# Softmax attention: maxima of four heads side by side in four PSUM banks, and the work between the scores dealt out anew

## The reference, cut to what matters

```python
q = (x @ w_q + b_q).reshape(B, Lq, 16, 32)          # x: 8 x 512 x 512
k = (context @ w_k + b_k).reshape(B, -1, 16, 32)    # context: 8 x 512 x 384
v = (context @ w_v + b_v).reshape(B, -1, 16, 32)
scores  = einsum('bqhd,bkhd->bhqk', q, k) / sqrt(32)
weights = softmax(scores, axis=-1)
out = einsum('bhqk,bkhd->bqhd', weights, v).reshape(B, Lq, 512) @ w_o + b_o
```

## Time and profile before

| | |
|---|---|
| median of 3 timed runs | 1717.89 us (1717.18 to 1721.56) |
| the profiled execution | 1716.18 us, its span 1713.9 us |
| softmax attention | from about 622 us to about 1420 us of the span |
| busy over the span | PE 92%, DVE 72%, ACT 66%, POOL 60% |
| mean granted TensorE clock | 0.977 of full |

### The profile page before, as it was taken

The page is one execution under the profiler, slowest core; times in us unless marked ns, Lnnn a source line. Parts: engine busy times, 40 slices in busy tenths (PEclk is TensorE's granted clock), DMA queues, the critical chain, the costliest instruction groups (busy, mean ns, idle before and its releaser), DMA issues. The chain is left out here.

```text
span 1713.9 us, 29296 instructions
## 1 busy us (share of the span) xinstructions
PE 1576.5 (92%) x8836; PEld 711.7 (42%) x8836; DVE 1225.9 (72%) x1756; ACT 1128.4 (66%) x1895; POOL 1023.3 (60%) x738
## 2 busy tenths in 40 slices
PE   5999878998999977999999999999999978999998
PEld 3545433444444432334344443444343413444443
DVE  4978898997989745776776767676767666665553
ACT  5667598887888744665656666666656566566562
POOL 4767437766677723565667566665757565554452
PEclk9989999999999997999999999999999999999999
DMA  8411000000000112121211212121211100010001
GB/s 313 143 66 42 1 1 1 1 1 1 0 1 1 62 52 73 33 59 26 58 33 38 54 29 57 26 57 32 58 25 40 55 25 25 25 49 24 24 24 49
DMA packets 61230, 72.21 MB, mean 42 GB/s; under 512 B 15312, under 2 KB 40784, under 8 KB 60624
## 3 DMA queue, kind: packets, MB, share of 16 engines
q1 hardware_dynamic: 56944, 62.22, 12.3%
q10 hardware_dynamic: 4192, 8.92, 1.3%
HBM read 37.40 MB, written 8.39 MB: 27 GB/s over the span
## 5 line engine op out<-in xcount | busy, mean ns | idle before, releaser
L1556 DVE TENSOR_REDUCE s_mx<-bank 128x1 f32<-128x512 f32 x512 | 336.9, 685 | 193.9 <-PE bank L1684 188.0
L1443 ACT ACTIVATE s_E<-bank 128x512 f32<-128x512 f32 x512 | 293.8, 595 | 195.4 <-PE bank L1696 171.9
L1342 POOL TENSOR_TENSOR s_E<-s_E 128x1024 f32<-128x1024 f32 x128 | 300.3, 2367 | 123.7 <-PE bank L1704 116.6
L1684 PE MATMUL bank<-s_KA,s_QA 96*128 96x512 f16 x512 | 193.3, 388 | 20.7 <-DMA s_KA<-sm_cx 10.4
L1696 PE MATMUL bank<-s_QA,s_KA 97*128 97x512 f16 x512 | 195.7, 384 | 3.9 <-ACT s_E L1443 1.4
L1335 POOL TENSOR_TENSOR sm_cx<-s_qkf,sm_cx 128x512 f16<-128x512 f32 x64 | 76.4, 1194 | 171.3 <-ACT sm_cx L1421 171.2
L1865 POOL TENSOR_TENSOR sm_cx<-m_xf,sm_cx 128x512 f16<-128x512 f32 x60 | 84.1, 1407 | 105.0 <-ACT sm_cx L1907 105.0
L1704 PE MATMUL bank<-s_E,s_V 128*32 128x512 f32 x1024 | 135.6, 602 | 3.9 <-ACT s_E L1443 3.9
L1075 PE MATMUL bank<-sm_zz,w1raw 128*128 128x512 f16 x256 | 99.7, 389 | 28.4 <-DVE sm_cx L962 15.4
L1098 PE MATMUL bank<-f_w2q,w2raw 128*128 128x512 f16 x512 | 121.8, 379 | 0.6 <-DVE w2raw L950 0.3
L772 POOL TENSOR_TENSOR sm_wkv<-sm_wkv,sm_cx 128x511 f32<-128x511 f32 x48 | 66.2, 1380 | 89.8 <-DVE sm_wkv L962 80.5
(11 more groups left out here) (264 smaller groups left out, 4055.1 us busy)
## 6 DMA issues: line engine op xcount, KB each, us to landing
sm_cx<-in_ctx SPq DMA_DIRECT2D x16, 768.0 KB, 4.6
s_QA<-sm_cx SPq DMA_DIRECT2D x384, 32.0 KB, 1.9
s_KA<-sm_cx SPq DMA_DIRECT2D x372, 32.0 KB, 1.9
X<-in_x SPq DMA_DIRECT2D x8, 1024.0 KB, 6.7
out_x<-X SPq DMA_DIRECT2D x8, 1024.0 KB, 4.3
w1raw<-in_w ACTq DMA_DIRECT2D x1, 4096.0 KB, 13.9
w2raw<-in_w ACTq DMA_DIRECT2D x1, 4096.0 KB, 27.3
w1raw<-in_wq SPq DMA_DIRECT2D x1, 1024.0 KB, 5.4
```

The costliest lines, as they stand in the source:

```text
L1342: e.tensor_tensor(into, into, other, ALU.add).then_inc(s_sum.sem, 1)
L1443: e.activation(E[:, SLOT[k] + h, :], SC[u % 2][:, :], ACT.Exp, scale=1.0 / float(np.sqrt(DH)))\
L1556: e.tensor_reduce(mx[:, h, q:q + 1], MX[q % 2][:, :], AX.X, ALU.max).then_inc(s_red.sem, 1)
L1684: e.matmul(MX[k % 2][:, :], QA[0:MROW, m, h, q * P:(q + 1) * P], KA[0:MROW, m, h, :], start=True, stop=True).then_inc(s_mx.sem, 1)
```

## The change

It is confined to the softmax attention.

1. **Maxima.** `maxima(b, m, q)` issues four matmuls, one for each head, that contract only over the 32 rows of the high halves, straight from `qkh` (now double buffered) rather than from the stacked `QA` and `KA`. They write banks 0 to 3. DVE reduces two banks at a time: 2 reductions of 128 x 2 x 512 for each query tile, 8 a group, where there were 16 of 128 x 512.
2. **Phases.** Banks 0 and 1 are also the score banks. So a group becomes four phases: when the four exponentials of a key tile are done, PE makes the next group's maxima of one query tile, DVE reduces banks 0 and 1, and then the scores of the next key tile may go. `attend` and `denominators` stand between maxima and scores.
3. **The maximum row** is transposed at the start of its own group rather than at unit 15 of the one before, and its DMA is issued by SP (`maximum_row`) and no longer by ACT.
4. **The rest** (`queries`, `values`, `output`, transposes, residuals, reciprocals, divisions, `summed`) is dealt out anew. Outputs are spread over `m == 1` and `m == 2`; the transposes go to units 9, 11, 13, 15.

```diff
-    SPARSE_K, SPARSE_V = (-1, 1, 3), (5, 7, 9, 12)
-    K_UNITS = (SPARSE_K, (-1, 0, 1), (2, 3, 4), SPARSE_K)
-    T_UNITS, STATS_UNITS = (4, 6, 8, 10), (1, 3, 6, 10)
-    RESIDUAL = {4: 0, 8: 1, 12: 2}
+    Q_AT = ((-1, -1, 1, 3), (-1, -1, 1, 3), (0, 1, 2, 3), (0, 1, 2, 3))
+    K_AT = ((3, 5, 7), (5, 7, 7), (7, 7.5, 11), (3, 3.5, 5))
+    T_AT = (9, 11, 13, 15)
+    O_AT = ({}, {3: ((0, 0),), 7.5: ((0, 1),), 11: ((0, 2), (0, 3)), 11.5: ((1, 0),), 13: ((1, 1),), 15: ((1, 2), (1, 3))},
+            {3: ((2, 0),), 5: ((2, 1),), 7: ((2, 2),), 9: ((2, 3),), 11: ((3, 0),), 11.5: ((3, 1),), 13: ((3, 2),), 15: ((3, 3),)},
+            {})
+    RES_AT = ({}, {12: 0}, {0: 1, 10: 2}, {0: 3})
...
+        SC, MX, MAXED, NUM, DEN, R6, R7 = banks[0:2], banks[0:4], pairs[0:2], banks[4], banks[5], banks[6], banks[7]
...
+            def maximum_row(b, m):
+                s_mrow.wait(e, b, m + 1)
+                s_sc.wait(e, b, 16 * (m + 1) - 16 * NG)
+                e.dma_start(QA[MROW:MROW + 1, m, :, :].rearrange("o h (q n) -> o (h q) n", n=P), mrow[:, :])\
+                    .then_inc(s_md[m].sem, 16)
+
             def step(b, m, first, last):
                 proj = what(b, m, first, last)[0]
                 if m == 0 and not last:
                     context(b + 1)
+                maximum_row(b, m)
                 if proj:
                     stack(e, *proj, 0)
                     stack(e, *proj, 1)
...
-            def maximum(b, m, k):
-                h, q = divmod(k, TT)
+            def maxima(b, m, q):
                 s_mT.wait(e, b, m)
-                s_mx.wait(e, b, 16 * m + k + 1)
-                e.tensor_reduce(mx[:, h, q:q + 1], MX[q % 2][:, :], AX.X, ALU.max).then_inc(s_red.sem, 1)
+                s_mx.wait(e, b, TT * m + q + 1)
+                for i in range(2):
+                    e.tensor_reduce(mx[:, 2 * i:2 * i + 2, q], MAXED[i][:, :, :], AX.X, ALU.max).then_inc(s_red.sem, 1)
...
+                s_red.wait(e, b, 2 * (TT * m + q))
+                high = qkh[m % 2]
+                for h in range(4):
+                    head = slice(h * DH, (h + 1) * DH)
+                    last = e.matmul(MX[h][:, :], high[head, 0, q * P:(q + 1) * P], high[head, 1, :], start=True, stop=True)
+                last.then_inc(s_mx.sem, 1)
...
+                if proj and Q_AT[m][0] < 0:
+                    queries(*proj, 0, 0)
+                rows(b, m)
+                between(-1)
+                for u in range(UNITS):
+                    t, h = divmod(u, 4)
+                    if nxt and h == 0:
+                        if t == 0:
+                            s_mrow.wait(e, b, m + 1)
+                        e.wait_ge(s_ex.sem, s_ex.count(b, 16 * m + 4 * t))
+                        maxima(*nxt, t)
+                    if t and h == 0:
+                        attend(b, m, t - 1)
+                    if div and u == 0:
+                        attend(*div, TT - 1)
+                        denominators(*div, 0)
+                    if div and u == 4 * DN_TILE[m]:
+                        denominators(*div, 1)
+                    between(u - 0.5)
+                    score(b, m, u, nxt)
+                    between(u)
```

More of the change, by code:

```diff
@@ L1367, in step @@
                     e.tensor_scalar(omu[:, :], mu[:, :], -1.0, 1.0, ALU.mult, ALU.add).then_inc(s_c, 1)
-                summed(b, m, 0, 0)
-                summed(b, m, 0, 1)
+                if m == 0:
+                    ln_p(e, b + 1)
+                if m != 2:
+                    summed(b, m, 0, 1)
+                if late and (m == 0 or m == 3 and not last):
+                    divided(*late)
                 if last and m == 3:
@@ L1486, in step @@
             def step(b, m, first, last):
-                proj, nxt, div = what(b, m, first, last)
-                if m == 2 and not last:
-                    for c in range(KC):
-                        context(b + 1, c)
-                if proj:
-                    queries(*proj, 0)
-                if div and N_UNIT[m] < 0:
+                proj, nxt, div, late = what(b, m, first, last)
+                rows(b, m)
+                if first and m == 0:
+                    e.wait_ge(s_lo, 2)
+                    e.wait_ge(s_raw[3], 32)
@@ L1494, in step @@
+                if m == 0 and not first:
+                    values(b, 1)
+                if m == 1:
+                    values(b, 3)
+                if m == 2 and not last:
+                    context(b + 1, 0)
+                    context(b + 1, 1)
+                if m == 3:
+                    divided(b, 0)
+                elif div:
                     numerators(*div)
+                if m == 2 and not last:
+                    context(b + 1, 2)
                 for u in range(UNITS):
-                    if u == UNITS - 1 and nxt:
-                        rows(*nxt)
@@ L1517, in _ @@
+                if last and m == 3:
+                    divided(b, 2)
             e.wait_ge(s_b, 32)
[L1518 removed]
+            queries(0, 0, 0, R6)
             queries(0, 0, 1)
@@ L1581, in step @@
             def step(b, m, first, last):
-                proj, nxt, div = what(b, m, first, last)
+                proj, nxt, div, late = what(b, m, first, last)
                 if last and m == 0:
                     s_res.wait(e, 1, 0)
-                if m == 2 and not first:
-                    residual(b - 1, TT - 1)
-                if nxt:
-                    for k in range(MAX_AHEAD):
-                        maximum(*nxt, k)
                 for u in range(UNITS):
-                    if m == 1 and not first and u in RESIDUAL:
-                        residual(b - 1, RESIDUAL[u])
-                    if m == 1 and not last and u - 1 in T_UNITS:
-                        low(b + 1, T_UNITS.index(u - 1), R7)
                     if last and m == 3:
@@ L1741, in step @@
             def step(b, m, first, last):
-                proj, nxt, div = what(b, m, first, last)
+                proj, nxt, div, late = what(b, m, first, last)
                 if m == 0:
-                    reader[6], reader[7] = (s_V, b, 2), (s_qkf, b, 4)
-                if m == 2 and nxt:
-                    for k in range(MAX_AHEAD):
-                        maximum(*nxt, k)
-                if proj:
-                    for c in range(KD):
-                        queries(*proj, 0, c)
@@ L1794, in _ @@
                     values(0, m, t, m)
-            for k in range(UNITS):
-                maximum(0, 0, k)
-            rows(0, 0)
             s_V.wait(e, 0, 2)
-            e.wait_ge(s_lo, 2)
+            for q in range(TT):
+                maxima(0, 0, q)
             steps(step, e)
```

241 lines of the change are left out of this document (124 added, 117 removed).

## The result

The changed kernel takes **1823.41 us** (median of 4 runs, 1821.8 to 1825.84); before, on the same chip, 1717.54. The ratio is 1.0614, interval [1.0591, 1.0637]: slower by 105.9 us. The direction was forecast, the size was not: 1783 had been predicted and 1823 lies 5 us above the range. The profiled execution has a span of 1823.0 us against 1713.9, with a mean granted clock of 0.950 against 0.977.

What follows compares the result with a forecast made beforehand. PE's instruction stream bounded the kernel at 93.75 us a batch; SP's queue and waits would make it 103.5. Six batches give +58, the last boundary -2.5, batch 0 +9: +65, forecast 1783 us, range 1706 to 1818.

Steps and rivals of the forecast that it cites:

- Maxima, 0.35 us a group, and reductions, 1.22 us: Four maxima matmuls on PE run partly side by side in 0.35 us; a DVE reduction of 1024 elements takes 1.22 us.
- Rival B: Maxima matmuls run one after another (0.97 us) or reductions take 1.37: +4 us a batch, 1815 us; chance 0.05.
- Rival A: PE's clock also falls behind the gaps before groups 3 and 0: 4 us a batch, 1811 us; chance 0.2.
- Phases without SP, 96.1 us: A batch's four groups without SP's queue: 22.4, 27.0, 23.9 and 22.8 us, together 96.1 us.
- Group 1, 27.0 us by the low halves: PE's transposed chunks wait in bank 7 for DVE's low halves, giving phases of 5.5, 5.4, 7.6 and 8.5 us.
- Group 2, 27.0 us by k's lateness on SP: k is taken only after unit 11, so SP's stackings end at 25.1 us and the row lands at 27.0.
- Groups 0 and 3, 22.9 and 26.6 us: The row waits behind 24 stackings on SP, in group 3 also behind the context load, and sets the groups' times.
- SP's start, S + 5.6 and S + 7.1: SP begins stacking 5.6 us (group 0) and 7.1 us (group 3) after S, the start of a phase's first score.
- the whole context term: Context load ahead of group 3's row on SP: 0.6 us to issue and 1.8 us later landing.
- Batch 0, +9: Batch 0, without outputs: groups of 22.9, 24.8, 26.2 and 26.6 us, 100.5 against some 91.
- Last batch 0 after -2.5, start 0: Last boundary without context load saves 2.5 us; last batch gains and loses 5 us; the first scores come no later.
- Rival C: SP's queue and bank 7's low halves don't hold PE: 91.4 us a batch, 1700 us; chance 0.16.

Runs made afterwards that it cites:

- e1: Changed kernel with the maximum row's DMA issued by ACT again instead of SP: 1722.4 us, 1.0046 of the kernel before.
- e6: Changed kernel with k of group 2 made behind units 5 and 7 and taken by ACT after unit 7 instead of 11: 1799.2 us.
- e3: Changed kernel with 16 (group 0) and 9 (group 3) extra unread matmuls in PE's gap before the row: 1809.4 us.
- e2: Changed kernel with the maximum row issued ahead of the context load on SP: 1799.9 us.
- e7: e5 with the row's transpose right behind score 15 and, at the end, POOL's last pair sums ahead of group 2's low half: 1699.6 us.
- e5: e1 with group 1's output chunks ahead of the transposed chunk of x on PE: 1709.0 us, 0.9984 of the kernel before.
- e9: e5 with DVE's four normalisations at units 0 to 3 of group 1 instead of 0, 1, 4 and 5: 1703.5 us.
- e11: e7 with group 2's transpose left where it was and the normalisations at units 0 to 3: 1698.4 us, 0.9905 of the kernel before.
- e4: Changed kernel with three of group 1's table entries moved (reciprocals, residual 0, first output chunk of query tile 1): 1839.3 us.
- e8: e5 with group 1's reciprocals at units 4 (two), 9 and 11 instead of 4, 8 (two) and 12: 1729.5 us.
- e10: e8 with DVE's four normalisations moved to units 0 to 3 of group 1: 1713.4 us, 0.9995 of the kernel before.

## Why the prediction was wrong in size, point by point

- **Maxima, 0.35 us a group, and reductions, 1.22 us: right.** 0.32 to 0.33 us to the next instruction, 1.221 us. Rival B is out. (Its time did not follow from its price: 4 us a batch give A's 1811, not 1815.)
- **Phases without SP, 96.1 us: right.** e1 gives 95.6. The single groups were off by 0.4 to 1.3 us with both signs.
- **Group 1, 27.0 us by the low halves: right in mechanism, 1.0 short.** It took 28.0. The lower clock behind PE's wait in bank 7 had not been counted: in batches 1 and 2, where the matmuls behind it stayed 0.22 us apart, group 1 took 26.7.
- **Group 2, 27.0 us by k's lateness on SP: right.** 26.9; e6 takes it away.
- **Groups 0 and 3, 22.9 and 26.6 us: here it failed.** They took 24.9 and 29.4. The step is SP's start, S + 5.6 and S + 7.1. It was worked out from matmuls at 0.22 us although the same part had put gaps of 3.8 and 3 us in front of these phases. SP started at S + 7.3 and, in group 3 of batch 2, at 967.68 - 959.13 = 8.55. e3 gives 5.56 as soon as the gap is filled, and e1, without gaps, 5.6 and 6.9. The row behind the context took 4.1 us to land where 3.6 had been taken; e2 prices the whole context term at 3.4 to 3.9 us a batch, where the prediction had 0.6 + 1.8.
- **Rival A was the case, not a rival.** It had 0.2 because PE "was little used before that one gap". That premise was weak, for PE was busy 6.3 of the 9 us before that gap (1380 to 1389). And here PE was busy 9.0 of the 9.2 us before the 5.2 us gap (974 to 983.2), and the clock falls all the same. A's 4 us a batch were about right (24.9 + 28.0 + 26.9 + 29.4 = 109.2 against 103.5, less 1.0 in group 1 and 0.5 in the landing). What put even its 1811 too low were these 1.5 us a batch, some 9 us over the loop, and batch 0.
- **Batch 0, +9: mis-sized, it is +20.5.** Its groups take 26.2, 27.8, 25.9 and 30.3 us where 22.9, 24.8, 26.2 and 26.6 had been taken. It has gaps of 2.3, 5.0 and 5.8 us in front of the first scores of groups 1 and 3 and of the next batch, and the lower clock behind them. The 7.2 us in front of its own first score are counted to the start.
- **Last batch 0 after -2.5, start 0: wrong.** +7.1 and -5.4. PE's 5.30 us at the very end wait for POOL's pair sums, whose move behind `divided(b, 2)` was in the code and had not been followed; e7, which makes the sums first, leaves 1.17. At the start PE waits 7.2 us for the first row, which stands on SP behind the stackings and the context (1.5 us in e1). The first score comes earlier than before all the same, since the first row is made at 649.4 instead of 658.0. How much of that is scatter no run shows.
- **Rival C, that SP and bank 7 don't hold: out.** With SP relieved (e1) and bank 7's wait filled (e5) the kernel is level with the one before; C's time needed what e7, e9 and e11 added, and was then met: 92.2 us a batch where C had 91.4, 1698 us where it had 1700.

The loop was 33 us more than predicted (88.6 for 58 - 2.5), batch 0 11.5 more, the last 7.1, less 5.4 and 1.7 at start and rest: 44.6, which with the predicted 64.5 is the 109.1 of the span. The direction was not luck: by e1 the row's place on SP's queue, which the forecast named, made some 97 of the 106 us, the lower clock behind its gaps included.

The rule of the Trainium skill (DMA: Bandwidth & Descriptors, Issuing engines are not separate DMA queues) that initiating DMAs on several engines saves only the sequencer's time, usually small, does not help here: e1 moves one DMA of 4 KB a group to another engine and gains some 97 us, because the sequencer needs 0.63 us for each of 24 DMAs ahead of it. The page's first half agrees: the transfers themselves are as fast on either, 1.7 us. The order in which descriptors of one queue start, which the prediction took from the same section, stands in the page's next one (Two DMAs through the same engine are not ordered).

## What to carry to other kernels

Before a latency-bound DMA changes its queue, add up the issue time of everything ahead of it in that queue and the time at which that begins: here 24 small DMAs of 0.63 us, started a quarter into the group, set the period. Where a count finds a gap on TensorE in front of work that others wait for, cost that work at the lower clock in the same sum, not as another case, since what is delayed there may make the next gap: in the changed kernel's loop all gaps of 3.4 to 6.2 us were followed by it. And where one engine waits for a late producer, first put its own independent work ahead of the wait (e5, -13 us). Moving the producer's work about cost 18 to 20 us (e4, e8), most of it, as e10 shows for e8, by a collision that the wait itself did not show.

## What the hardware showed that was not expected

- **DVE is held by POOL.** A normalisation of 128 x 512 fp32 from SBUF to SBUF takes 0.45 to 0.54 us when it starts with POOL idle and up to 2.59 us when it starts during a POOL instruction; it ends 0.3 us after that one does (e5 and e8). e9 and e10 show the cost, 5 and 16 us. The Trainium skill (SBUF — State Buffer, Who interferes with whom) describes one port pair that the two engines share under an exclusive lock, which `tensor_scalar` can take in a two-port mode; the traces agree in that one engine's instruction waits out the other's, while no row shows the mode. It also says that reductions don't contend, and the 1.22 us ones never stretched (1.23 us is the longest of 256 in the changed kernel).
- **Short waits on PE can be followed by the lower clock, and not always are.** In e1 six matmuls ran at 1.2 GHz behind a wait of 1.31 us in four batches and none in another; a wait of 1.20 us in the same group was always followed by matmuls 0.22 us apart. In e2 two of six gaps of some 3.5 us were followed by full clock. No run here shows what decides it. Filling 3.6 us of a gap with matmuls that nobody reads made the program faster.
- **Four 32-row matmuls into four banks cost about 0.33 us** from first start to the next instruction, 0.87 if they ran one after another.
